# The inverse root in the second attention of a two-layer gated block: one GpSimd power operation in place of eleven DVE operations

## The reference

```python
B, S1, S2, DCA = (2, 256, 128, 16)
QDIM, KDIM, H = (256, 128, 16)
HD = QDIM // H            # 16
EPS = 1e-06
def _ln(t, w, b):
    m = jnp.mean(t, axis=-1, keepdims=True)
    v = jnp.var(t, axis=-1, keepdims=True)
    return (t - m) * jax.lax.rsqrt(v + EPS) * w + b
q = _ln((x @ Wq + bq).reshape(b, s1, H, HD), qn_w, qn_b)
k = _ln(kv[..., :HD], kn_w, kn_b)
k_dca = _ln(kv_dca[:, :, 0], kn_dca_w, kn_dca_b)
x = x + jnp.tanh(g_xattn[1]) * _L1_xattn_ref(_layernorm(x), ctx_1024, ...)
```

## Time and profile before

| what | us |
| --- | --- |
| median of 3 runs | 1356.01 (1355.36 to 1357.71) |
| span of the profiled execution, first to last instruction | 1354.8 |
| PE busy in it | 1046.2 (77%) |
| DVE busy | 765.6 (57%) |
| ACT busy | 424.9 (31%) |
| POOL busy | 307.7 (23%) |

### The profile page before, as it was taken

The page is one execution under the profiler, slowest core; times in us unless marked ns, Lnnn a source line. Parts: engine busy times, 40 slices in busy tenths (PEclk is TensorE's granted clock), DMA queues, the critical chain, the costliest instruction groups (busy, mean ns, idle before and its releaser), DMA issues.

```text
span 1354.8 us, 16681 instructions
## 1 busy us (share of the span) xinstructions
PE 1046.2 (77%) x5397; PEld 863.6 (64%) x5397; DVE 765.6 (57%) x1687; ACT 424.9 (31%) x781; POOL 307.7 (23%) x271
## 2 busy tenths in 40 slices
PE   3989989989885700578772377877879999999997
PEld 2867867868663500467661246464757989899896
DVE  6367567585658889323226897786865324242221
ACT  3554445374533300112120032323252232322321
POOL 0413304223000000577771182630200000000000
PEclk8999989999986755788786565768676989899899
DMA  7008600000000140477765640100000000000001
GB/s 264 1 0 288 211 1 0 0 0 1 1 0 20 39 129 1 142 213 223 213 196 185 245 157 32 64 0 0 0 0 1 1 1 0 0 0 0 0 0 62
DMA packets 63667, 91.24 MB, mean 67 GB/s; under 512 B 5901, under 2 KB 56327, under 8 KB 60807
## 3 DMA queue, kind: packets, MB, share of 16 engines
q1 hardware_dynamic: 56116, 71.42, 16.3%
q0 software_dynamic: 6144, 18.88, 4.5%
q10 hardware_dynamic: 1363, 0.37, 0.1%
HBM read 60.74 MB, written 29.89 MB: 67 GB/s over the span
## 4 chain that ended last, share of the span: by engine, by line
PE 55%; DVE 20%; issue 10%; ACT 5%; POOL 4%; DMA 4%; ACTq 1%; DVEq 0%; POOLq 0%; SPq 0%
PE bank L1993 12%; PE bank L2012 7%; PE bank L1651 4%; PE bank L1696 4%; DMA xg<-table,src_now 3%; PE bank L1921 3%; PE bank L1681 2%; PE bank L1879 2%; PE bank L2004 2%; DVE y_sum L1170 2%; PE bank L1798 2%; PE bank L1938 2%; PE bank L1811 2%; POOL q_lo L481 2%; DVE cand L946 1%
## 5 line engine op out<-in xcount | busy, mean ns | idle before, releaser
L1993 PE MATMUL bank<-gu_hi,xnT_split 128*128 128x352 f32 x640 | 159.5, 329 | 0.0
L481 POOL TENSOR_TENSOR q_lo<-soft,q_hi 128x512 fp32r<-128x512 f32 x64 | 93.2, 1456 | 250.2 <-ACT soft L1355 249.9
L1993 PEld LDWEIGHTS bank<-gu_hi,xnT_split 128*128 128x128 f32 x640 | 113.3, 191 | 1.0 <-issue 0.7
L492 POOL DMA_INDIRECT xg<-table,src_now x64 | 62.4, 975 | 222.4 <-DVE src_now L971 203.2
L1233 DVE SCALAR_TENSOR_TENSOR soft<-sg,combine_w,bank 128x176 f32<-128x176 f32 x160 | 56.5, 394 | 88.2 <-PE bank L1993 82.6
L1993 PE MATMUL bank<-gu_lo,xnT_split 128*128 128x352 f32 x320 | 104.2, 325 | 0.0
L2012 PE MATMUL bank<-dn,attnT 128*128 128x256 f32 x448 | 101.2, 384 | 0.0
L751 DVE COPY qT<-bank 128x512 f32<-128x512 f32 x64 | 44.2, 690 | 85.9 <-PE bank L1696 84.8
L2012 PEld LDWEIGHTS bank<-dn,attnT 128*128 128x128 f32 x448 | 85.5, 194 | 11.2
L671 DVE SCALAR_TENSOR_TENSOR x<-bank,gates,x 128x256 f32 (+1 forms) x48 | 22.8, 482 | 114.6 <-PE bank L2012 95.2
L1553 ACT ACTIVATE sg<-bank 128x352 f32<-128x352 f32 x80 | 37.2, 465 | 153.6 <-PE bank L1993 153.6
(11 more groups left out here) (259 smaller groups left out, 2261.6 us busy)
## 6 DMA issues: line engine op xcount, KB each, us to landing
y<-zeros SPq DMA_DIRECT2D x16, 1024.0 KB, 10.8
y_rows<-y SPq DMA_DIRECT2D x16, 1024.0 KB, 4.8
w_gu<-in_L_ffn_w_gu SPq DMA_DIRECT2D x32, 352.0 KB
w_dn<-in_L_ffn_w_down SPq DMA_DIRECT2D x32, 176.0 KB
gu<-in_L_gu SPq DMA_DIRECT2D x1, 3520.0 KB, 12.9
table<-xw SPq DMA_DIRECT2D x4, 640.0 KB
wq<-in_L_xattn_Wq SPq DMA_DIRECT2D x1, 2048.0 KB, 12.6
wo<-in_L_xattn_Wo SPq DMA_DIRECT2D x1, 2048.0 KB, 20.5
```

Source lines behind the costliest of these rows:

```text
L481: pool.tensor_tensor(q2_lo[:, h % 3, :], q2[h % 2], q2_hi[:, h % 3, :], ALU.subtract).then_inc(q2_split, 1)
L492: pool.indirect_dma_start(xg[:, q, e, :], None, table, bass.IndirectOffsetOnAxis(ap=src_now[:, q, e:e + 1], axis=0)).then_inc(xg_loaded[q] ...
L1993: mm = pe.matmul(b[:, 0:2 * F1], v[:, c, j * P:(j + 1) * P], w[:, c, p, o, :], start=(n == 0), stop=(n == len(terms) - 1))
```

## The change

`deviation` on DVE keeps the sum and the variance, signals POOL, and waits for POOL's signal. POOL raises the 128 x 80 variances to the power of -0.5 with one `tensor_tensor`, its second operand a tile filled with -0.5, just ahead of `affine_queries` of the same group. `inverse_root` stays as it is for all other callers.

```diff
@@ tiles and semaphores
+        minus_half = sb("minus_half", [P, QK])
+        q1_variance = sem("q1_variance")
+        q1_root = sem("q1_root")
@@ POOL
+            def roots(i):
+                pool.wait_ge(q1_variance, i + 1)
+                pool.tensor_tensor(qk1_stat[:, 1, :], qk1_stat[:, 0, :], minus_half[:], ALU.pow).then_inc(q1_root, 1)
...
             pool.memset(ctx1T[:], 0.0).then_inc(mask_step, 1)
+            pool.memset(minus_half[:], -0.5).then_inc(mask_step, 1)
+            pool.wait_ge(mask_step, 5)
+            roots(0)
             affine_queries(0)
             key_blocks(0)
             pool.wait_ge(y2_used, 2 * G)
             with pool.Fori(1, NG - 1) as i:
                 combine(i + 1)
+                roots(i)
                 affine_queries(i)
                 key_blocks(i)
+            roots(NG - 1)
             affine_queries(NG - 1)
             key_blocks(NG - 1)
@@ DVE, deviation(i)
                 ch.add(dve.tensor_reduce(qk1_stat[:, 0, :], qk1_sq[:], AX.X, ALU.add))
                 ch.wait()
-                ch.add(dve.tensor_scalar(qk1_stat[:, 0, :], qk1_stat[:, 0, :], 1.0 / D1, EPS1, ALU.mult, ALU.add))
-                ch.wait()
-                inverse_root(qk1_stat[:, 1, :], qk1_stat[:, 0, :], QK)
+                dve.tensor_scalar(qk1_stat[:, 0, :], qk1_stat[:, 0, :], 1.0 / D1, EPS1, ALU.mult,
+                                  ALU.add).then_inc(q1_variance, 1)
+                dve.wait_ge(q1_root, i + 1)
...
-            FRONT_CHAIN = NORMED_CHAIN + 1 + 2 + ROOT_CHAIN + 2
+            FRONT_CHAIN = NORMED_CHAIN + 1 + 1 + 2
```

## The result

The changed kernel takes 1398.02 us (median of 4 runs, 1397.03 to 1401.11) against 1355.68 us before (4 runs): ratio 1.0315, 95% interval 1.0286 to 1.0344. It is slower, as forecast, but by 42 us and not by 4: ten times the forecast, and outside the range of 1348 to 1376.

A forecast was written before the change was run, and what follows sets the result against it. It took DVE's chain at four roots as the bound: 3.86 + 0.14 - 2.99 = +1.01 us each, 4.0 in all, so the 1354.8 us span becomes 1358.8, and the median 1360.0 us; range 1348 to 1376.

The forecast's parts named there:

- The price of the power: POOL's new operation at each root: estimated 3.86 us, between a low end of 0.47 and a high end of 10.3.
- 22 steps inside one instruction at POOL's price a number: Middle estimate of the POOL power: two halves, each about eleven steps, at 2.02 ns a number, 3.86 us.
- The high end: Dearest estimate of the POOL power: 22 steps, each costing a whole 80-number addition of 0.47 us, 10.3 us.
- The sentence from the skill on dependent chains: Skill page: 4 cycles a number per dependent fp32 step; 5.9 us for 22 steps, kernel about 1368 us, kept beside the sum.
- What goes: DVE's eleven Newton operations at each of four roots: 2.99 us removed each, DVE's busy time down 10.3 us.
- The handoffs: DVE to POOL 0.08 us and POOL to the next engine 0.06 us, together 0.14 us at each root.
- What of it reaches the end: Group 0 and attentions 0, 1 and 2: a DVE delay counts in full four times, 4 x 1.01 = +4.0 us.
- The caps of the cheap case: Gains in attentions capped by PE's idle 1.72, 2.34, 2.61 us before `contexts(2)`; 8.8 us gained at a 0.47 us power.
- a cheap power: Rival, chance 34%: the POOL power takes under 2.17 us and the kernel gets faster, down to 1347.2 us.
- The queue ahead of the power: POOL's `combine` ends before the variances are ready, with 13 us of cover at the closer one, so it delays nothing.
- The clock: PE's granted clock changes around `contexts(2)`: plus or minus 3.5 us, widening all cases without being one itself.
- The case of a power of 6 us or more: Very dear power at the four roots, chance 12%: 12.6 us or more lost, at the high end 1385.8 us.

The follow-up runs named there:

- the product: Against the changed kernel, POOL's one instruction multiplies the variance by -0.5 instead of raising it to the power; 1344.23 us against 1353.7, ratio 0.9923.

## Why the prediction was right in its direction and wrong in its size

- **The price of the power.** This step failed: "22 steps inside one instruction at POOL's price a number", 3.86 us; it is 13.16. The sum had one unknown term, and it was mis-sized by a factor of 3.4. The high end, "each step costs as much as a whole addition of 80 numbers", 10.3 us, was no bound either, since it kept the guessed count of 22 while only the price of a step was raised. In rows: a number costs 159 ns, 79 times the 2.02 ns of an addition. At that price a step it would be 79 steps and not 22; whether there are more steps or dearer ones no run shows. The count came from how DVE does the root, which says nothing of how POOL's routine does it: the same root by twelve plain POOL instructions takes 5.09 us. The sentence from the skill on dependent chains gave 5.9 us for the same 22 steps: nearer, still under half.
- **What goes.** 2.99 us a root; DVE's busy time fell from 765.6 to 755.3 us, the 10.3 us that were worked out. Right.
- **The handoffs.** 0.14 us forecast, 0.12 us with the product and 13.35 - 13.17 = 0.18 us with the power. Right.
- **What of it reaches the end.** All four roots in full, with no slack: 10.3 us at the first maximum and at each `contexts(2)`. Right. With the measured 13.16 the same formula gives 4 x (13.16 + 0.14 - 2.99) = 41.2 us, against 42.3 measured.
- **The caps of the cheap case.** 8.8 us forecast for an instruction of 0.47 us, 9.5 measured with 0.354. Right, with help from the clock: two of the three `contexts(2)` ran 1.5 and 1.3 us shorter. The case itself, a cheap power, was given 34% and was far off.
- **The queue ahead of the power.** POOL had been idle for 15.84 and 13.63 us when the variances of groups 1 and 2 came; `combine` was not in the way. Right.
- **The clock.** A swing of up to 3.5 us was allowed for; in the changed kernel all three `contexts(2)` took 3.62 us, against 3.62, 3.45 and 3.62 before, so none came from there.
- **The chances.** Slower was given 50%. The sign turns at a power of 2.85 us, and the 3.86 us that put the sum above it came from a count of steps with no row behind it, so the right direction owes something to luck. The case of a power of 6 us or more had 12%, and its high end, 1385.8 us, lay below what was measured. With one term bounded from one side only, the range should have been open on the dear side.

## What to carry to other kernels

A power on POOL costs about 0.42 us and 0.16 us a number and partition, so with its handoffs it beats this Newton chain on DVE only below some 10 numbers, an estimate from two sides: at 16 wide the chain takes 2.4 us and the power by that price 3.0 and its handoffs, at 4 wide the stretch is 2.2 against 1.2 to 1.3. Count what an engine waits for, not how many instructions it gets rid of: eleven short operations on the path were four times cheaper than one long one. And where an operation isn't in the trace, an estimate by steps isn't an upper bound; one look at it by itself is worth more than the rest of the sum.

## What the runs showed of the hardware that was not expected

- The power is linear in the numbers, and costs the same for both exponents tried: 1.03 us for 4, 6.79 for 40, 10.59 for 64 and 13.16 for 80, and 13.16 with an exponent of 1.
- It did not stretch DVE's operations beside it, while plain products on POOL held small DVE operations until they had ended: 128x4 operations of 0.16 us took 0.96 beside products of 1.04 us, and one of 0.17 us took 2.19 beside a product of 2.35.
- Plain POOL operations of 80 numbers take 0.25 to 0.35 us, less than the 0.47 us that a straight line through 256 and 1024 numbers gives.
